# GpSimd's order for the first chunks: chunk 3's gathers behind the low part of chunk 0's half tile of layer 1, those of chunks 4 and 5 one place later

## What is computed

```python
e = jnp.stack([tbl_0[ids[:, 0]], ..., tbl_38[ids[:, 38]]], axis=1)      # 512 x 39 x 16
x0 = xk = e
for idx, (W, b) in enumerate(params):                                  # W: 39 x fk x 128
    z = jax.nn.relu(jnp.einsum('bhd,bkd,hks->bsd', x0, xk, W) + b[None, :, None])
    if idx != n_layers - 1:
        xk = z[:, :64, :]; direct.append(z[:, 64:, :])
    else:
        direct.append(z)
z = jnp.sum(jnp.concatenate(direct, axis=1), axis=-1)                  # 512 x 256
h = jnp.concatenate([z, dense_ctx], axis=1)                            # 512 x 272
h = jnp.maximum(h @ W_top1 + b_top1, 0.0)
h = jnp.maximum(h @ W_top2 + b_top2, 0.0)
y = h @ W_top3
```

## Time and profile before

| | |
|---|---|
| Time before, median of 3 runs | 679.48 us (672.77 to 683.57) |
| Span of the profiled execution, first to last instruction | 674.9 us |
| PE busy | 638.7 us (95%) |
| DVE busy | 588.5 us (87%) |
| ACT busy | 253.3 us (38%) |
| POOL busy | 314.3 us (47%) |
| Mean granted clock of PE over the span | 0.992 |
| GpSimd's gathers, L333 | x160, mean 1052 ns |
| GpSimd's low parts of half tiles, L351 | x32, mean 1362 ns |

### The profile page before, as it was taken

How to read it: one execution, slowest core, us unless ns; L and a number is a source line. 1 busy time by engine, 2 the same in 40 slices (tenths; PEclk the granted TensorE clock), 3 DMA queues, 4 the chain that set the end, 5 groups by cost and what they waited for, 6 DMA issues and landing times.

```text
span 674.9 us, 6021 instructions
## 1 busy us (share of the span) xinstructions
PE 638.7 (95%) x1878; PEld 350.3 (52%) x1878; DVE 588.5 (87%) x550; ACT 253.3 (38%) x331; POOL 314.3 (47%) x392
## 2 busy tenths in 40 slices
PE   0777899999999999999999999999999999999998
PEld 0334455555555555555555555555555555555554
DVE  0258598999999999999999999999999999999950
ACT  1122324444444344343344443443433434433322
POOL 6775655436455453546364454536364132122320
PEclk9999699999999999999999999999999999999999
DMA  9689826985757759393857568583948476090200
GB/s 199 171 257 347 236 97 200 286 323 140 259 181 217 246 151 311 73 336 85 317 139 251 194 180 282 149 304 68 341 94 289 155 230 221 13 298 1 68 0 2
DMA packets 126751, 130.12 MB, mean 193 GB/s; under 512 B 60734, under 2 KB 68686, under 8 KB 126719
## 3 DMA queue, kind: packets, MB, share of 16 engines
q1 hardware_dynamic: 117743, 128.23, 59.0%
q0 software_dynamic: 5120, 1.32, 2.1%
q10 hardware_dynamic: 3856, 0.18, 0.4%
HBM read 123.31 MB, written 6.39 MB: 192 GB/s over the span
## 4 chain that ended last, share of the span: by engine, by line
PE 86%; POOL 2%; issue 2%; DMA 2%; DVE 1%; ACT 0%; DVEq 0%; ACTq 0%; POOLq 0%
PE z L677 55%; PE z L667 9%; PE z L668 8%; PE z L669 8%; DMA bc<-fields 2%; POOL emb L333 2%; PE z L684 1%; PE z L685 1%; PE z L750 1%; DVE low L585 1%; PE top L740 1%; DVE raw L601 0%; PE tp L740 0%; PE z L740 0%; PE xk L756 0%
## 5 line engine op out<-in xcount | busy, mean ns | idle before, releaser
L677 PE MATMUL z<-whole,w 128*128 128x512 f32 (+2 forms) x928 | 428.8, 595 | 1.7 <-DVE whole L609 1.0
L677 PEld LDWEIGHTS z<-whole,w 128*128 128x128 f32 (+2 forms) x928 | 175.4, 190 | 157.9 <-issue 140.4
L609 DVE TENSOR_TENSOR whole<-bc,xk 128x1024 f32<-128x1024 f32 (+1 forms) x208 | 231.5, 1134 | 21.5 <-PE z L677 11.6
L436 ACT ACTIVATE high<-raw 128x1024 fp32r<-128x1024 f32 (+1 forms) x128 | 135.4, 1059 | 295.4 <-DVE raw L601 239.0
L333 POOL DMA_INDIRECT emb<-in_tables,rows_all x160 | 168.2, 1052 | 57.4 <-issue 52.4
L585 DVE TENSOR_TENSOR low<-raw,high 128x1024 fp32r<-128x1024 f32 (+1 forms) x128 | 161.5, 1262 | 9.1 <-ACT high L436 9.1
L667 PE MATMUL z<-high,w_high 128*128 128x512 f32 (+1 forms) x256 | 143.7, 561 | 6.6 <-DVE low L585 4.6
L601 DVE TENSOR_TENSOR raw<-bc,xk 128x1024 f32<-128x1024 f32 x112 | 136.0, 1214 | 0.0
L351 POOL TENSOR_TENSOR stack<-stack_raw,stack 64x512 fp32r<-64x512 f32 x32 | 43.6, 1362 | 190.1 <-ACT stack L443 184.0
L668 PE MATMUL z<-high,w_low 128*128 128x512 f32 (+1 forms) x256 | 101.7, 397 | 0.0
L669 PE MATMUL z<-low,w_high 128*128 128x512 f32 (+1 forms) x256 | 101.4, 396 | 0.0
(11 more groups left out here) (61 smaller groups left out, 198.9 us busy)
## 6 DMA issues: line engine op xcount, KB each, us to landing
bc<-fields SPq DMA_DIRECT2D x64, 1024.0 KB, 6.8
rot<-fields SPq DMA_DIRECT2D x16, 1280.0 KB
bc<-fields SPq DMA_DIRECT2D x16, 768.0 KB
rot<-fields SPq DMA_DIRECT2D x16, 512.0 KB
fields<-xt SPq DMA_DIRECT2D x64, 80.0 KB
bc<-fields SPq DMA_DIRECT2D x32, 128.0 KB
rep<-fields SPq DMA_DIRECT2D x48, 80.0 KB
emb<-in_tables,rows_all POOLq DMA_INDIRECT x160
```

Of the source, the lines that this page charges most:

```text
L436: act.activation(high[0:m, k % PART_SLOTS], raw[0:m, k % RAW_SLOTS], ACT.Copy).then_inc(high_ready, 1)
L609: nc.vector.tensor_tensor(whole[0:rows, n % WHOLE_SLOTS, 0:len(tiles)], left, right, ALU.mult).then_inc(whole_ready, 1)
L677: ins = nc.tensor.matmul(z[layer][:, :], w[layer][0:m, WHOLE_AT[layer, t], :], whole[0:m, k % WHOLE_SLOTS, u], start=(t == 0), stop=(layer ...
```

## The change

GpSimd's order alone. All instructions stay the same in number and in what they compute, and the other engines' programs don't change.

```diff
-            for c in range(4):
+            for c in range(3):
                 gather(c)
+            landed(1)
             landed(2)
-            landed(3)
             fold(0, 0)
             stack_part(1, 0)
             own_done()
-            gather(4)
-            landed(4)
+            gather(3)
+            landed(3)
             fold(1, 0)
             fold(0, 1)
             stack_part(2, 0)
             own_done()
-            gather(5)
-            landed(5)
+            gather(4)
+            landed(4)
             stack_part(1, 1)
             fold(0, 2)
             fold(1, 1)
             for p in range(1, CHUNKS + 1):
-                if p > 1 and p + 4 in IN:
+                if p + 4 in IN:
                     own_done()
                     gather(p + 4)
                     landed(p + 4)
                 fold(2, p - 1)
```

## The result

The changed kernel takes 680.4 us (median of 12 runs, 678.0 to 689.3). The kernel before, run beside it, takes 678.1 us (12 runs, 672.8 to 688.8). The ratio is 1.0052, 95% interval 1.0027 to 1.0076: 3.5 us slower, where 6.1 us faster was forecast. By 2% it is no difference. Measured again later it was 1.0045 (1.0012 to 1.0078). The kernel before against itself, though, came out at 1.0059 (1.0010 to 1.0109).

What follows compares the result with a forecast made beforehand. PE, busy for 95% of the span, was taken as a continuous stream behind 60 us with one hole, at (1,0). -7.0 + 0.5 + 0.4 = -6.1 us took the median from 679.5 to 673.4; 8 in 10 range 669.5 to 681.

Steps and rivals of the forecast that it cites:

- The hole at (1,0): PE's wait for GpSimd's low part at (1,0) goes: 7.0 us won, 5.7 from the wait, 1.3 from the clock.
- PE's next wait for low: At (0,1), PE waits about 2 us for DVE's low, ending near 69.6, with the clock not falling.
- the first place: The part of the change that acts at (1,0), removing PE's wait there: 7.0 us won.
- Transfers asked for earlier: Rot of chunk 2 may come late for DVE's raw of (0,2): cost 0.5 us, between 0 and 1.4.
- The middle gathers: Chunk 3's and 4's gathers land before the low parts of (2,0) and (1,1) can be made: nothing charged.
- The place (1,2): Chunk 5's gathers now precede the low part of (1,2), ready at 141.6 against PE's 141.23: cost 0.4 us.
- the quiet case: Landing of chunk 5's gathers ahead of (1,2) taken as 1.71 us, as in the steady part, not 5.24 or 5.93.
- my 4.0 us: PE idle time after which the clock was still full; the fall at (1,2) was expected from about 4.0 us on.
- The slower one: At (1,2), PE waits 4.6 us, then loses 4.6 at half clock: +2.7 us, 682.2; chance 0.14.
- a late landing with the clock held: At (1,2), PE waits 3.9 us without a clock fall: -2.6 us, 676.9; chance 0.16.

Runs made afterwards that it cites:

- the second place alone: Kernel before with only chunk 5's gathers moved behind fold (1,1), ahead of fold (2,0) and the low part of (1,2); ratio 1.0116, 7.9 us slower.
- the filler: Three extra matmul pairs, result unused, ahead of (0,0)'s split group; against the plain kernel before: kernel before with them 1.0027, changed kernel with them 1.0051.
- rot held: Changed kernel, with SyncE's load of chunk 4's rot waiting until chunk 5's gathers have landed; 673.5 us, ratio 0.9986 to the kernel before.
- the split: Changed kernel with seven of chunk 5's gathers behind fold (1,1), three behind fold (1,2); ratio to the kernel before 0.9989 (676.3 us), again 0.9944 (672.1 us).
- the split with the filler: Changed kernel with chunk 5's gathers split seven and three, plus extra matmuls ahead of (0,0)'s split group; ratios to the kernel before 0.9962 and 0.9977.

## Why the prediction was wrong

**The hole at (1,0).** The mechanism was right: the wait went, with GpSimd 3.3 us early (low part over at 65.68, PE at 68.94); PE's next wait for low was 2.53 us (2 forecast) and left the clock at 1.00; from A to the split group of (2,0) it took 80.98 - 68.94 = 12.0 us, where 77.0 - 64.73 = 12.3 was forecast and 19.4 stood before. Thus the 7.0 us were true of the execution that I read. **They were not true of the kernel.** The step that failed is the tacit one: taking one execution's wait as every execution's. PE's arrival is set by the start (64.4 to 71.5 us over the profiles, and 78.1 in one), GpSimd's by how fast 40 gathers go (57.3 us from the first to the end of the last in the kernel before, 55.6 in its repeat, 53.4 with the second place alone, 57.5 with the filler); the wait was 4.96 in one profile of the kernel before, 0.96 in the next. The timed runs put the first place at 2.6 us (changed without chunk 5's gathers against before) to 4.4 (7.9 for the second place alone, less 3.5 for both), with intervals of some 2.4 and 3.7 us to either side. The spread of 10.8 us between the three runs was a sign of it, and I used it only to widen the range.

**Transfers asked for earlier.** 0.5 was taken, from 0 to 1.4. In the profiled execution it was 0: no wait for low at (0,2). With a quick start it is real: PE waited 1.54 us there in the changed kernel with the filler, just beyond my bound, and rot was late again at (0,3), which I had not counted (in the profiled execution that cost PE 0.75 us, about as much as the 0.86 in the kernel before).

**The middle gathers** cost nothing, as forecast: the low part of (2,0) waited for ACT, not for GpSimd.

**The place (1,2).** Here is the term that was mis-sized, 0.4 us against 5.1 (B to C). From the end of ACT's direct half (116.80) to PE's half tile I had summed 21.0 us; it took 24.4:

| Step | forecast | measured |
|---|---|---|
| fold (1,1) | 2.0 | 2.8 (first add 1.49 us) |
| to the first gather | 0.76 | 0.48 |
| ten gathers | 13.0 | 13.9 |
| landing | 1.71 | 3.69 |
| fold (2,0) | 2.0 | 2.1 |
| low part | 1.44 | 1.26 |

The landing is the largest. I had read the DMA share of 0.42 in one window as nearer to the quiet case; rot's load then began 0.3 us after the last gather was issued (133.46 and 133.16). The experiment with rot held gives 1.47 back. The other 1.3 us came from taking typical durations for a chain with no slack at all: what two steps gained here (0.3 and 0.2 us) does not make up for the others. The clock then added 1.6, more than nothing and less than the 4.6 of the rival, since it was at 0.50 for 3.4 us only. In the profiled execution it fell to 0.50 at about 141 us, 3.3 us after PE had stopped, and in the one with the second place alone 2.2 us after; my 4.0 us as the point from which it falls was read from one case and was too high.

From PE's restart at (1,2) to the clock's return went 3.2, 4.9, 5.7 and 3.6 us (changed, again, second place alone, filler at the start), and B to C, less the 16.0 without a wait and less the wait, was 1.6, 2.5, 2.8 and 1.8 us, half of it each time; PE waited for nothing in these stretches. At (1,0), where PE waited for DVE within the slow stretch, the 9.2 us cost 1.3 by my estimate from rows 4 and 6.

The landing of chunk 5's gathers ahead of (1,2) (of the first seven in the split) took 3.6 to 4.6 us at a DMA share of 0.87 to 1.05, against 1.5 at 0.05 to 0.21 and 2.0 at 0.55.

**The rivals.** The slower one, late landing and a fallen clock, is what happened: forecast +2.7 with 0.14, measured +3.5. It was reached with a smaller loss at (1,2) (5.1 in place of 9.2) and a smaller gain at (1,0). Its chance was too low: all three gathers of the first 120 us had landed in 4.5 us or more, and these were the nearest rows to a place where SP is about to load, nearer than the steady part. That 680.4 us lies inside the range of 669.5 to 681 is no merit of the account: the upper bound was set for a late landing with the clock held, and the direction was wrong.

**What stays open.** The start's own scatter (A) was not explained; the traces lead part of the way. PE's split group of (0,0) waits for DVE's low, DVE for ACT's rounding, and this stands in ACT's queue behind the copy of chunk 1's turned rows. That copy in the kernel before, in the changed kernel again, and in the first profile of the split with the filler (its line is L427 there, its execution took 687.8 us):

```profile
36.65 0.28 ACT L422 ACTIVATE xt<-tp 128x128 f32<-128x128 f32 x1 [15.58 <-issue]
39.62 0.28 ACT L422 ACTIVATE xt<-tp 128x128 f32<-128x128 f32 x1 [18.94 <-remote]
46.29 0.28 ACT L427 ACTIVATE xt<-tp 128x128 f32<-128x128 f32 x1 [25.30 <-remote]
```

PE then waited 3.11, 6.49 and 9.62 us for the low of (0,0), and A was 64.7, 69.4 and 78.1. PE's transposes for this copy were over by 37.0 us in all three; what held ACT beyond them the trace does not name. It is not all of the scatter: the second place alone has A at 70.1 with this copy at 36.49. Open too is whether the loss in the times is 3.5 us or close to nothing, since two measurements of one kernel came out 0.6%, 4 us, apart.

## What to carry to other kernels

A wait between two engines that run free of each other is a difference of two arrival times; before pricing its removal, ask how much each of them scatters, and take a second profile if there is one. Work with a blocking wait that is moved out of one gap must be costed in its new gap with late values of every step, above all a transfer's landing next to another queue's burst (3.69 us here, 1.47 with the burst held back). If it doesn't fit, cut it to the size of the gaps (seven and three gathers here), or hold back the burst that collides with it; both took the wait away here, while a gain in time over the kernel before was measured for the first alone, and in one of two measurements.

## What the runs showed of the hardware

- Chunk 5's ten gathers took 13.9 us to issue in the changed kernel, 14.7 in the one with the filler at the start, against 13.0 for chunk 6's in the kernel before.
- Ahead of (1,2), chunk 5's gathers (in the split the first seven) landed in 1.46 to 1.55 us at a DMA share of 0.05 to 0.21 and in 2.01 at 0.55, and in 3.56 to 4.63, at 0.87 to 1.05, where a rotation's load began between 1.7 us ahead of the start of the last gather and 0.4 us behind it. The longest landing was 6.0 us, at a share of 0.97 (chunk 5's in the kernel before with the filler). The share alone does not set it: chunk 6's took 1.73 us at 0.64 in the changed kernel and 1.71 at 0.25 in the kernel before.
- The granted clock went from 1.00 to 0.50 after 4.0 us of idle PE at (1,0) in the kernel before, and at (1,2) after 3.3 us in the changed one, 3.1 in its repeat and 2.2 with the second place alone. It stayed at 0.50 for 10.2 us at (1,0), and at (1,2) for 3.4, 6.8 and 6.8. The idle 2.53 us ahead of low of (0,1) left it at 1.00 in the changed kernel, but with rot of chunk 4 held it went to 0.50 after an idle of 2.40 us ahead of low of (0,3), 1.3 us after PE had gone on.
- At a clock of 0.50 the matmuls of the split group of (0,1) in the kernel before start 0.43 us apart (76.39, 76.82, 77.25), at 1.00 those of (2,0) 0.23 us apart (85.01, 85.24, 85.47).
- GpSimd's first add of fold (1,1) took 1.49 us in every profile in which GpSimd had waited for ACT's direct half there, the repeat of the kernel before among them, and 0.74 in the one profile in which it had not. Why was not looked into.
